# Integrator of a two-layer block in double chunks of 1024 columns, with tanh written into SBUF

## The reference

```
attn = attn @ out_w + out_b
x = x + attn
ctx = attn.reshape(b * s, d)
xs = _ln(x, g1, b1).reshape(b * s, d)
vs = jnp.zeros_like(xs)
def step(carry, _):
    xs, vs = carry
    u = jnp.tanh(ctx @ w_ctx + xs @ w_x + b_inl)
    vn = vs + DT * (u - xs - vs)
    xn_ = xs + DT * vn
    return ((xn_, vn), None)
(xs, vs), _ = jax.lax.scan(step, (xs, vs), None, length=NUM_ITERS)   # 8 steps, DT = 0.1
x = x + xs.reshape(b, s, d)
h = _ln(x, g2, b2)
h = jax.nn.gelu(h @ ff_w1 + ff_b1, approximate=False)
```

## Time and profile before

| | us |
|---|---|
| median of 3 runs | 1121.7 (1120.17 to 1123.55) |
| profiled execution, its own time | 1115.86 |
| profiled execution, span | 1114.1 |
| first matmul of the integrator (L478), from the span's start | 353.03 |
| first matmul of the norm behind it (L300) | 446.36 |
| first matmul of the feed-forward part (L494) | 466.20 |

### The profile page before, as it was taken

One profiled execution on the slowest core, in us unless ns is written; L12 is line 12 of the kernel. 1 busy time (PEld: TensorE's weight loads), 2 busy tenths in 40 slices (PEclk: granted clock), 3 DMA queues, 4 the chain that ended last, 5 costly groups with the idle time before them and its releaser, 6 DMA issues.

```text
span 1114.1 us, 20198 instructions
## 1 busy us (share of the span) xinstructions
PE 970.9 (87%) x6976; PEld 583.2 (52%) x6976; DVE 630.8 (57%) x2018; ACT 539.3 (48%) x952; POOL 451.6 (41%) x681
## 2 busy tenths in 40 slices
PE   7788889888868986898988996589997999999995
PEld 4366666666643221343634994256663644366664
DVE  2578888888813989322543442467772643344443
ACT  4626566666645544644412663347774422233331
POOL 1136677667530999000055552025551064022231
PEclk9879999999988999999899997779998899999997
DMA  6500000000020000300012243000000012011115
GB/s 212 189 1 3 2 2 2 2 2 2 2 86 0 1 1 0 151 0 0 1 39 67 73 147 90 0 1 1 2 1 1 1 41 65 0 35 43 42 30 162
DMA packets 31872, 41.91 MB, mean 38 GB/s; under 512 B 6880, under 2 KB 26720, under 8 KB 30912
## 3 DMA queue, kind: packets, MB, share of 16 engines
q1 hardware_dynamic: 27232, 31.26, 8.9%
q0 software_dynamic: 4544, 9.38, 2.6%
HBM read 29.16 MB, written 16.66 MB: 41 GB/s over the span
## 4 chain that ended last, share of the span: by engine, by line
PE 46%; DVE 4%; ACT 3%; POOL 3%; issue 3%; DMA 1%; SPq 0%; DVEq 0%; POOLq 0%
PE PS L599 5%; PE PS L577 5%; PE PS L581 5%; PE PS L300 3%; PE PS L533 3%; PE PS L535 3%; POOL sorted_rows L1451 3%; PE PS L542 2%; PE PS L494 2%; PE PS L499 2%; PE PS L590 2%; PE PS L681 2%; PE PS L700 2%; PE PS L711 2%; PE PS L668 2%
## 5 line engine op out<-in xcount | busy, mean ns | idle before, releaser
L799 ACT ACTIVATE pw<-PS 128x768 f32<-128x768 f32 x128 | 103.8, 811 | 90.3 <-PE PS L414 89.1
L1394 POOL TENSOR_SCALAR_AFFINE_SELECT pw<-pw 128x256 f32<-128x256 f32 x256 | 104.9, 434 | 94.1 <-ACT pw L799 92.2
L1028 DVE CUSTOM_DVE_ANT_0 PS<-PS,above 128x256 f32<-128x256 f32 x256 | 115.9, 453 | 42.1 <-PE PS L389 38.7
L1457 POOL DMA_INDIRECT token_rows<-xnb,slot_in x78 | 74.9, 960 | 158.8 <-ACT xnb L889 158.8
L1266 DVE TENSOR_TENSOR rsb<-sqb,PS 128x256 f32<-128x256 f32 (+1 forms) x78 | 43.2, 554 | 112.2 <-ACT sqb L882 99.4
L392 PE MATMUL PS<-kf,qm 32*128 32x256 f32 x512 | 92.6, 449 | 5.8 <-DVE mx L1030 3.8
L1444 POOL TENSOR_TENSOR XS<-XS,N 128x512 f32<-128x512 f32 x64 | 80.1, 1296 | 30.7 <-DVE N L1102 27.3
L1004 DVE TENSOR_TENSOR xnb<-PS,rsb 128x512 f32<-128x512 f32 x56 | 38.7, 691 | 88.4 <-ACT rsb L768 66.3
L1416 POOL TENSOR_SCALAR_AFFINE_SELECT pw<-pw 128x256 f32<-128x256 f32 x128 | 55.8, 471 | 72.5 <-ACT pw L919 72.5
L1030 DVE CUSTOM_DVE_ANT_0 PS<-PS,above 128x128 f32<-128x128 f32 x256 | 84.6, 331 | 0.0
L1451 POOL DMA_INDIRECT sorted_rows<-H,pos x32 | 30.9, 967 | 129.1 <-DVE pos L1247 119.7
(11 more groups left out here) (206 smaller groups left out, 2399.3 us busy)
## 6 DMA issues: line engine op xcount, KB each, us to landing
sorted_rows<-empty_rows_dram SPq DMA_DIRECT2D x2, 2535.0 KB, 14.8
slot_in<-sorted_rows SPq DMA_DIRECT2D x78, 65.0 KB, 1.9
N<-token_rows SPq DMA_DIRECT2D x16, 256.0 KB, 4.9
X<-xT_dram SPq DMA_DIRECT2D x4, 512.0 KB, 6.5
ATT<-gate_dram SPq DMA_DIRECT2D x1, 2048.0 KB
XS<-down_dram SPq DMA_DIRECT2D x1, 2048.0 KB
H<-up_dram SPq DMA_DIRECT2D x1, 2048.0 KB
out_dram<-X SPq DMA_DIRECT2D x8, 256.0 KB, 3.0
```

The lines of the kernel that those rows point to most:

```text
L799: nc.scalar.activation(pw[:, w % 2, j:j + 2, :], PS[:, A_PST:A_PST + 2, 0:3 * P], ACT.Exp).then_inc(a_p, 1)
L1028: nc.vector.tensor_tensor_reduce(PS[:, j, 0:SEQ], PS[:, j, 0:SEQ], above[:, :], 1.0, -3e38, ALU.add, ALU.max, mx[:, 1, j, g:g + 1])
L1394: m = nc.gpsimd.affine_select(x[:, :, SEQ * k:SEQ * k + P], x[:, :, SEQ * k:SEQ * k + P], [[0, 2], [1, P]], ALU.is_ge, 0.0, base=0, channe ...
L1457: nc.gpsimd.indirect_dma_start(token_rows[l][:, :], bass.IndirectOffsetOnAxis(slot_in[:, r, D:D + 1].bitcast(mybir.dt.int32), 0), slot_out ...
```

## The change

A unit is now a pair of chunks, 1024 columns (`PAIRS` = 4). There are 32 pair steps q, and all four pairs go through each step together; the two halves are gone. PE's sums take all eight PSUM banks, two matmuls for each pair, with one count behind the second. ACT, DVE and POOL each do a pair in one instruction. As no bank is left, tanh goes to SBUF: `pulls` is four buffers of 1024 columns in `sqb` and `rsb`, which the norms use otherwise. The `drive` and `velocity` instructions read and write these. Each `settle` is a pair, all four stand at the end, and each chunk of the norm waits on PE for its own pair.

```diff
+        pulls = [t[:, 2 * n:2 * n + 2, :] for t in (sqb, rsb) for n in range(2)]
+        PAIRS = NCH // 2
...
-            sp.wait_ge(i_h, NCH)
+            sp.wait_ge(i_h, PAIRS)
...
+            for q in range(STEPS * PAIRS):
+                n, w = q // PAIRS, q % PAIRS
+                if n:
+                    pe.wait_ge(i_v, q - PAIRS + 1)
+                for c in (2 * w, 2 * w + 1):
+                    s = slice(c * CH, (c + 1) * CH)
+                    if n == 0:
+                        nc.tensor.matmul(PS[:, c, :], wctx[:, :], ATT[:, s], start=True, stop=False)
+                        m = nc.tensor.matmul(PS[:, c, :], wxs[:, :], XS[:, s], start=False, stop=True)
+                    else:
+                        m = nc.tensor.matmul(PS[:, c, :], wxs[:, :], V[:, s], start=False, stop=True, skip_group_check=True)
+                m.then_inc(i_p, 1)
...
-            pe.wait_ge(i_h, NCH)
-            ln(LN_G2, H)
+            ln(LN_G2, H, lambda k: pe.wait_ge(i_h, k // 2 + 1))
...
-                nc.scalar.activation(PS[:, 4 + q % 4, :], PS[:, q % 4, :], ACT.Tanh, bias=col(C_INL)).then_inc(i_u, 1)
+                nc.scalar.activation(pulls[w], PS[:, 2 * w:2 * w + 2, :], ACT.Tanh, bias=col(C_INL)).then_inc(i_u, 1)
...
-                m = nc.vector.scalar_tensor_tensor(out=PS[:, 4 + k, :] if n else V[:, s], in0=XS[:, s], scalar=-DT * DT,
-                                                   in1=PS[:, 4 + k, :], op0=ALU.mult, op1=ALU.add)
+                if q >= PAIRS:
+                    dve.wait_ge(i_x, q - PAIRS + 1)
+                nc.vector.scalar_tensor_tensor(out=pulls[q % PAIRS] if q >= PAIRS else wide(V, q), in0=wide(XS, q),
+                                               scalar=-DT * DT, in1=pulls[q % PAIRS], op0=ALU.mult,
+                                               op1=ALU.add).then_inc(i_d if q >= PAIRS else i_v, 1)
...
+                dve.wait_ge(i_d, q - PAIRS + 1)
+                nc.vector.scalar_tensor_tensor(out=wide(V, q), in0=wide(V, q), scalar=1.0 - DT, in1=pulls[q % PAIRS],
+                                               op0=ALU.mult, op1=ALU.add).then_inc(i_v, 1)
...
+            for q in range(STEPS * PAIRS):
+                drive(q)
+                if q > PAIRS:
+                    velocity(q - 1)
+            velocity(STEPS * PAIRS - 1)
+            for w in range(PAIRS):
+                settle(w)
...
+            for q in range(STEPS * PAIRS):
+                s = slice(2 * (q % PAIRS) * CH, 2 * (q % PAIRS + 1) * CH)
                 pool.wait_ge(i_v, q + 1)
                 nc.gpsimd.tensor_tensor(XS[:, s], XS[:, s], V[:, s], ALU.add).then_inc(i_x, 1)
```

More of the change, by code:

```diff
@@ L835, in _ @@
             ln(LN_G1)
-            for q in range(STEPS * NCH):
+            for q in range(STEPS * PAIRS):
+                w = q % PAIRS
                 act.wait_ge(i_p, q + 1)
-                if q >= 4:
-                    act.wait_ge(i_v, q - 3)
-                nc.scalar.activation(PS[:, 4 + q % 4, :], PS[:, q % 4, :], ACT.Tanh, bias=col(C_INL)).then_inc(i_u, 1)
+                if q >= PAIRS:
+                    act.wait_ge(i_v, q - PAIRS + 1)
+                nc.scalar.activation(pulls[w], PS[:, 2 * w:2 * w + 2, :], ACT.Tanh, bias=col(C_INL)).then_inc(i_u, 1)
             nc.scalar.preload_act_table_set(LN_EXP)
@@ L1090, in _, with wide @@
             ln(LN_G1, XS, g1s[:, 0:1], g1s[:, 1:2])
-            def step_of(q):
-                return q // (4 * STEPS), q // 4 % STEPS, q % 4
+            def wide(x, q):
+                w = q % PAIRS
+                return x[:, 2 * w * CH:2 * (w + 1) * CH].rearrange("p (c t) -> p c t", c=2)
             def drive(q):
-                half, n, k = step_of(q)
-                s = slice((4 * half + k) * CH, (4 * half + k + 1) * CH)
                 dve.wait_ge(i_u, q + 1)
-                if n:
-                    dve.wait_ge(i_x, q - 3)
-                m = nc.vector.scalar_tensor_tensor(out=PS[:, 4 + k, :] if n else V[:, s], in0=XS[:, s], scalar=-DT * DT,
-                                                   in1=PS[:, 4 + k, :], op0=ALU.mult, op1=ALU.add)
-                m.then_inc(i_d if n else i_v, 1)
@@ L1106, in velocity @@
-            def velocity(q):
[L1107 to L1117, removed]
+                if q >= PAIRS:
+                    dve.wait_ge(i_x, q - PAIRS + 1)
@@ L1118, in settle @@
+            def settle(w):
+                dve.wait_ge(i_x, PAIRS * (STEPS - 1) + w + 1)
+                nc.vector.scalar_tensor_tensor(out=wide(H, w), in0=wide(XS, w), scalar=DT * DT, in1=wide(H, w),
                                                op0=ALU.mult, op1=ALU.add).then_inc(i_h, 1)
-            for q in range(STEPS * NCH):
-                if q == 4 * STEPS:
+            for q in range(STEPS * PAIRS):
+                drive(q)
+                if q > PAIRS:
                     velocity(q - 1)
[L1123 to L1133, removed]
+            velocity(STEPS * PAIRS - 1)
+            for w in range(PAIRS):
+                settle(w)
+            dve.wait_ge(i_h, PAIRS)
             ln(LN_G2, N, col(C_G2), col(C_B2))
@@ L1438, in _ @@
             residual(BATCH - 1)
-            for q in range(STEPS * NCH):
-                c = 4 * (q // (4 * STEPS)) + q % 4
-                s = slice(c * CH, (c + 1) * CH)
+            for q in range(STEPS * PAIRS):
+                s = slice(2 * (q % PAIRS) * CH, 2 * (q % PAIRS + 1) * CH)
                 pool.wait_ge(i_v, q + 1)
```

## The result

The changed kernel takes 1169.0 us (median of 6 runs, 1161.5 to 1175.36) against 1120.93 us for the kernel before on the same chip (6 runs). The ratio is 1.045, 95% interval 1.041 to 1.049: it is slower by 48 us. Of the profiled executions, 1167.2 stands against 1115.86 us.

A forecast was written before the change was run, and what follows sets the result against it. DVE and POOL, side by side at about 1.23 us a chunk step, were taken to bound the integrator. Taking turns moves the norm's start from 446.4 to 505.3, +58.9 on 1121.7: 1180.6 us, range 1168 to 1194.

The forecast's parts named there:

- turns with the slopes' sizes: Integrator: DVE and POOL alternate, with instruction lengths from width slopes; 1173 to 1187 us, chance 74%.
- What bounds it before: Old integrator: DVE and POOL run side by side at nearly one pace, about 1.23 us a chunk step.
- tanh into SBUF turns overlap into turns: Drives and velocities get two SBUF inputs and take turns with POOL's additions, 4.59 us a pair.
- Rival 1: Integrator: no exclusion, drives and velocities go on beside POOL, which bounds; 1115 us, chance 8%.
- rival 2: Integrator: part exclusion; if half of DVE's 67 us stays beside POOL, about 1150 us; chance 6%.
- Width, DVE: Drive and velocity at doubled width: 1.13 us a pair from the slope, at most 1.20.
- Width, POOL: Addition at doubled width: 2.33 us a pair from the slope, between 2.19 and 2.47.
- Hidden: Steady part: rounds of three pairs, 7.0 us POOL then 6.8 us DVE; PE and tanh stay hidden, adding nothing.
- rival 3: Integrator: turns with upper POOL and DVE sizes and PE falling to 1.2 GHz; +10, 1190 us, chance 12%.
- signs named for the trace: Integrator trace: additions about 2.4 us, DVE and POOL busy near the stage's 152 us, norm's first matmul about 505.
- Start: Integrator's start: first tanh waits for a pair, at 359.45; drive 3 starts at 371.0, behind POOL's third addition.
- Settle and wait: Integrator's end: settle 0 ends 1.13 us behind POOL's last addition, at 505.3; the finer wait gives back 1.2 us.

The follow-up runs named there:

- experiment 1: The kernel before with only tanh moved into SBUF buffers of 512 columns, read by drive and velocity: 1224.7 us against 1159.5, ratio 1.053.
- experiment 2: The changed kernel with drive and velocity taking their second operand from PSUM sums: 1155.2 us against 1159.5 for the kernel before, ratio 0.994.
- Experiment 3: The changed kernel with GpSimd's addition replaced by a memset that reads nothing: 1156.5 us, stage 82.3 us.
- experiment 7: The changed kernel with the drive's second operand from PSUM sums and the velocity's still from SBUF: 1187.8 us, stage 119.5 us.
- experiment 6: The changed kernel with each 1024-column addition made as two of 512, both released by the same count: 1215.6 us, stage 140.6 us.
- experiment 8: The changed kernel with PE waiting for all four settles ahead of the norm: 1224.3 us, stage 149.0 us.

## Why the prediction was right, and where it was off

The forecast was 1180.6 us, +58.9; measured was +48.1, and +51.3 between the profiled executions. The sign, the cause and the range held. The median of 1169.0 lies only 1.0 us above the range's lower end of 1168, and below the 1173 to 1187 that the prediction gave to turns with the slopes' sizes: the turns were the mechanism, and the time was overstated by 10.8 us.

- *What bounds it before*, and *tanh into SBUF turns overlap into turns*: right. Experiments 1 and 2 show it from both sides: the SBUF operand alone makes 149.0 us of the stage, its removal alone 89.9. Experiment 3 narrows the cause to POOL's reads. Rival 1 is out, and so is rival 2 in its form "half stays overlapped": in 4.42 = 2 x 1.14 + 2.14 at most 0.2 us of POOL's 2.33 can have run beside DVE.
- *Width, DVE*: 1.13 us from the slope, 1.14 measured. *Width, POOL*: 2.33 from the slope is the free pace, and experiment 2 has 2.32. In turns it costs 2.14. The turn was mis-sized by 0.17 us (4.59 against 4.42); over the 28 pair steps behind the start that is 4.8 us. The 1.0 us put on top for changes of turn does not show, since 4.42 has them in it.
- *Hidden*: the rounds of three were wrong. Measured are rounds of one: the waiting velocity gets in behind every addition. The sum does not care, and PE and ACT are hidden in both: DVE shows no idle time in 110 us, and tanh is done ahead of the drives, though PE's clock fell to a mean of 0.82, and the cost that rival 3 gave this does not show. Two of the signs named for the trace failed with the rounds: additions last 3.26 us and not 2.4, as they are held too, and POOL is busy for 79.30 of 110.00 us and not throughout, since it waits 1.16 us in each turn for the next velocity.
- *Start*: drive 3 started at 369.25 and not 371.0, 1.7 us earlier: PE had full clock at the stage's start where before it had 0.50. That is luck, since experiments 2 and 7 had the clock of before at the same place. The drives of step 0 started behind their tanh, every 3.43 us, and not behind POOL.
- *Settle and wait*: the prediction had settle 0 behind POOL's last addition. It came in ahead of it, one addition of 2.1 us earlier. The reading that the prediction took from the Trainium skill, one instruction and not a run of them, was the right one at this place, and the 1178 given for it was the better number. Settle 1 was held by the last addition, and the four settles were over 5.5 us behind the norm's start, not 3.4, still ahead of DVE's first multiply.

Together 4.8 + 1.0 + 1.7 + 2.1 = 9.6 us, where the norm's first matmul came 9.4 us ahead of the forecast 505.3. The norm was 0.4 us shorter, 2.2 us were lost behind it, and the medians lie 3.2 us closer together than the profiled executions, which is spread of runs: 9.4 + 0.4 - 2.2 + 3.2 = 10.8 us.

## What to carry to other kernels

Before an operand of VectorE is moved from PSUM to SBUF, count the instruction's SBUF tensor inputs and ask whether GpSimd reads SBUF beside it: from one input to two, their times add up (here, for 1024 columns: 2.32 us side by side, 4.42 in turns, 3.41 with all three passes on VectorE). One or two instructions of the old kernel that already have the new form tell it, if their longest duration is read beside the median. And a wait for all parts in front of a stage that takes them one by one is worth looking at by itself: here it was the useful part of the change, 5.5 us in the changed kernel and, taken down to single chunks, about 7 us of 1162 on the kernel before. Before a gain of a few us is read from two profiles, compare the granted clock at the start of the stage: here it moved the stage by 2.7 us with no change of code.

## What the runs showed of the hardware

- The way can be held for longer than one instruction. A POOL that ran freely kept it over its next instructions: settles lasted 2.23 and 3.34 us, over one and two boundaries between additions, and 6.22 us in experiment 2, over two. Once POOL's instruction had itself been held, DVE got in at the next boundary, also ahead of a POOL instruction that was already released (experiment 6, and the last two additions of the changed kernel and of experiments 1, 7 and 8). What decides between the two was not tried and stays open.
- POOL's addition of 1024 columns takes 2.14 us of the turn when it is held at its start and 2.37 when it is not (experiment 7). That its start-up is hidden in the hold is a reading, not shown by a run of its own.
